# Lattice attention on one core: the product of sine and Gauss term moved to VectorE, all normalisations on GpSimd, and a head's steps laid out on 88 places

## What is computed

```python
scores = einsum('bhqd,bhkd->bhqk', q, k) / sqrt(D_K)      # 64 heads, 1024 x 1024, D_K = 64
int_scores = (abs(scores) * 1618.0).astype(int32)
scores = scores * where(int_scores % 9 in (0, 3, 6), 1/PHI, 1.0)
attn = softmax(scores)
attn = attn * (sin(C1 * attn) * exp(-attn * attn / PHI) + cos(C2 * attn))
ctx = einsum('bhqk,bhkd->bhqd', attn, v)
```

## Time and profile before

| | |
|---|---|
| median of 3 runs | 5791.73 us (5791.23 to 5793.92) |
| profiled execution | 5820.83 us, span 5819.0 us |
| busy, share of the span | PE 82%, DVE 71%, ACT 69%, POOL 65% |
| granted PE clock, mean | 0.944 |

### The profile page before, as it was taken

How to read it: one execution, slowest core, us unless ns; L and a number is a source line. 1 busy time by engine, 2 the same in 40 slices (tenths; PEclk the granted TensorE clock), 3 DMA queues, 4 the chain that set the end, 5 groups by cost and what they waited for, 6 DMA issues and landing times. The chain is left out here.

```text
span 5819.0 us, 98405 instructions
## 1 busy us (share of the span) xinstructions
PE 4780.6 (82%) x27646; PEld 2687.0 (46%) x27689; DVE 4160.0 (71%) x7651; ACT 3990.3 (69%) x5494; POOL 3775.7 (65%) x3599
## 2 busy tenths in 40 slices
PE   2788888888888888888888888888888869996999
PEld 1344444444444444444444444444444436554666
DVE  3677777777777777777777777777777656666665
ACT  1677777777777777777777777777777734444332
POOL 4677777777777777777777777777777634443233
PEclk8899999999999999999999999999999879998999
DMA  1000000000000000000000000000000000000000
GB/s 20 9 8 9 8 10 8 8 8 8 8 8 8 8 8 8 9 8 10 8 8 8 8 8 8 8 8 8 9 8 10 3 9 2 2 2 15 3 6 8
DMA packets 34205, 45.42 MB, mean 8 GB/s; under 512 B 24521, under 2 KB 24585, under 8 KB 34058
## 3 DMA queue, kind: packets, MB, share of 16 engines
q1 hardware_dynamic: 32010, 43.49, 2.8%
q0 software_dynamic: 2048, 0.14, 0.1%
HBM read 39.40 MB, written 4.19 MB: 7 GB/s over the span
## 5 line engine op out<-in xcount | busy, mean ns | idle before, releaser
L617 PE MATMUL banks<-ident,att 128*128 128x128 f32 x8192 | 1145.5, 287 | 408.6 <-DVE ag L549 247.1
L617 PEld LDWEIGHTS banks<-ident,att 128*128 128x128 f32 x8192 | 940.7, 147 | 1003.0 <-DVE ag L549 617.4
L659 PE MATMUL banks<-kT,qT 128*128 128x512 f32 x2048 | 1144.1, 658 | 275.8 <-DVE mx L578 266.5
L419 POOL TENSOR_TENSOR sinb<-sinb,ag 128x1024 f32<-128x1024 f32 x512 | 1280.7, 2505 | 82.7 <-ACT sinb L490 68.9
L569 DVE SCALAR_TENSOR_TENSOR mag<-near,mag 128x512 f32<-128x512 int32 x1024 | 859.6, 844 | 479.3 <-POOL near L435 470.6
L429 POOL TENSOR_SCALAR mag<-mag 128x512 f32<-128x512 f32 x1024 | 689.2, 677 | 567.7 <-DVE mag L569 533.7
L676 PE MATMUL outp<-work,vo 128*64 128x512 f32 x2048 | 1043.4, 634 | 0.0
L676 PE MATMUL outp<-sinb,vo 128*64 128x512 f32 x2048 | 1043.4, 634 | 0.0
L435 POOL TENSOR_SCALAR near<-mag 128x512 int32<-128x512 f32 x1024 | 796.4, 778 | 354.2 <-ACT mag L508 291.5
L508 ACT ACTIVATE mag<-banks 128x512 f32<-128x512 f32 x1024 | 598.7, 592 | 278.0 <-PE banks L659 276.4
L526 DVE TENSOR_TENSOR work<-banks,work 128x1024 f32<-128x1024 f32 x512 | 625.3, 1221 | 190.3 <-ACT work L484 187.7
(11 more groups left out here) (198 smaller groups left out, 6362.8 us busy)
## 6 DMA issues: line engine op xcount, KB each, us to landing
x<-xT_dram SPq DMA_DIRECT2D x128, 256.0 KB, 3.5
xT_dram<-xT SPq DMA_DIRECT2D x8, 256.0 KB
out<-hres SPq DMA_DIRECT2D x8, 256.0 KB, 2.6
base<-in_L_tok_turns,idx POOLq DMA_INDIRECT x64
wqk<-in_L_attn_Wq SPq DMA_DIRECT2D x64, 16.0 KB
wqk<-in_L_attn_Wk SPq DMA_DIRECT2D x64, 16.0 KB
wqk<-in_L_attn_bq SPq DMA_DIRECT2D x64, 0.2 KB
wqk<-in_L_attn_bk SPq DMA_DIRECT2D x64, 0.2 KB
```

Source lines behind the costliest of these rows:

```text
L419: nc.gpsimd.tensor_tensor(sinb[:, k % RING], sinb[:, k % RING], ag[:, k], ALU.mult).then_inc(tmul, 1)
L617: mm = nc.tensor.matmul(turn_pair(k)[:, c, i * P:(i + 1) * P], att[:, p, 4 * half + i, kt * P:(kt + 1) * P], ident[:], is_transpose=True, ...
L659: nc.tensor.matmul(score_bank(n), qT[:, p, (n // 2) * P:(n // 2 + 1) * P], kT[:, p, (n % 2) * 512:(n % 2 + 1) * 512], start=True, stop=Tru ...
```

## The change

The product goes from POOL to DVE. Rows 3 and 7 are normalised by POOL as the others, so `weights2` and `DVE_ROWS` are gone and the transposes wait on `weights` alone. Places are halved: STEPS is 88, and every list and offset is new. The square and the exponential of a Gauss column block and the `ag` product have offsets of their own (SQ, GEXP, AG). Instructions, shapes and buffers stay the same otherwise.

```diff
@@ -300,28 +300,28 @@
         outp = ctx.enter_context(nc.psum_tensor("outp", [P, 512], F32))
 
         names = ("consts loadq loadv projd qk_sb vald v_sb qk mags rounded kept factor filtered bias expd "
-                 "recip weights weights2 turned xpose squared gauss agd cosd acd nned sined tmul av evac folded "
+                 "recip weights turned xpose squared gauss agd cosd acd nned sined tmul av evac folded "
                  "outd").split()
         (consts, loadq, loadv, projd, qk_sb, vald, v_sb, qk, mags, rounded, kept, factor, filtered, bias,
-         expd, recip, weights, weights2, turned, xpose, squared, gauss, agd, cosd, acd, nned, sined, tmul,
+         expd, recip, weights, turned, xpose, squared, gauss, agd, cosd, acd, nned, sined, tmul,
          av, evac, folded, outd) = (sem("l_" + n) for n in names)
 
         NTILE = 2 * TB
         NX = 2 * TB
         HALF = TB // 2
-        STEPS = 44
-        SCORE = [0, 1, 6, 8, 10, 13, 15, 18, 19, 21, 26, 28, 29, 33, 35, 38]
-        ABS, RND, KEEP, FACT, FILT, BIAS = 1, 1, 2, 3, 4, 6
-        EXP = [STEPS + o for o in [4, 5, 7, 8, 9, 13, 15, 16]]
-        GAUSS = [STEPS + o for o in [12, 13, 15, 17, 18, 20, 22, 26]]
-        SINE = [STEPS + o for o in [28, 30, 32, 35, 36, 39, 41, 43]]
-        AV = [STEPS + o for o in [34, 37, 39, 42, 49, 51, 53, 58]]
+        STEPS = 88
+        SCORE = [0, 3, 7, 21, 23, 28, 34, 37, 40, 45, 51, 57, 60, 66, 72, 75]
+        ABS, RND, KEEP, FACT, FILT, BIAS = 2, 2, 5, 6, 9, 23
+        EXP = [STEPS + o for o in [12, 14, 15, 17, 18, 24, 26, 32]]
+        GAUSS = [STEPS + o for o in [24, 25, 30, 31, 38, 41, 43, 46]]
+        SQ, GEXP, AG = 2, 3, 5
+        SINE = [STEPS + o for o in [55, 58, 65, 67, 75, 80, 85, 88]]
+        AV = [STEPS + o for o in [68, 80, 82, 86, 96, 97, 101, 111]]
         OUT = (AV[HALF - 1] + 1, AV[-1] + 1)
-        FOLD, ADD = OUT[1] + 1, OUT[1] + 2
-        PROJ, VAL, EV = (17, 23), 31 + STEPS, 2
-        COS, MUL, RED, SIN, P3 = 1, 1, 3, 3, 4
-        NORM, TURNS = 1, 3
-        DVE_ROWS = (TB // 2 - 1, TB - 1)
+        FOLD, ADD = OUT[1] + 1, OUT[1] + 3
+        PROJ, VAL, EV = (36, 57), 61 + STEPS, 2
+        COS, MUL, RED, SIN, P3 = 1, 2, 6, 6, 9
+        NORM, TURNS = 2, 8
 
         block = ctx.enter_context(nc.Block())
 
@@ -412,13 +412,7 @@
             def iteration(t, par):
                 for s in range(STEPS):
                     for g, p, a in stages(t, par, s):
-                        if a - P3 in SINE:
-                            k = SINE.index(a - P3)
-                            wait(pool, sined, TB * g + k + 1)
-                            wait(pool, agd, TB * (g + 1))
-                            nc.gpsimd.tensor_tensor(sinb[:, k % RING], sinb[:, k % RING], ag[:, k],
-                                                    ALU.mult).then_inc(tmul, 1)
-                        if a - NORM in EXP and EXP.index(a - NORM) not in DVE_ROWS:
+                        if a - NORM in EXP:
                             j = EXP.index(a - NORM)
                             held(pool, recip, TB * g + j + 1)
                             nc.gpsimd.tensor_scalar(att[:, p, j], att[:, p, j], rs[:, j:j + 1], TURN,
@@ -491,8 +485,8 @@
                                                  scale=2.0 * math.pi * (1.0 - 2.0 ** -22)).then_inc(sined, 1)
 
                     for g, p, a in stages(t, par, s):
-                        if a - 1 in GAUSS:
-                            d = GAUSS.index(a - 1)
+                        if a - SQ in GAUSS:
+                            d = GAUSS.index(a - SQ)
                             wait(act, xpose, NX * g + d + 1)
                             if d < RING:
                                 wait(act, av, TB * g - RING + d + 1)
@@ -507,8 +501,8 @@
                             wait(act, filtered, NTILE * g + n - 3)
                             nc.scalar.activation(mag[:, n % 4], score_bank(n), ACT.Abs).then_inc(mags, 1)
                     for g, p, a in stages(t, par, s):
-                        if a - 1 in GAUSS:
-                            d = GAUSS.index(a - 1)
+                        if a - GEXP in GAUSS:
+                            d = GAUSS.index(a - GEXP)
                             wait(act, squared, TB * g + d + 1)
                             nc.scalar.activation(work[:, d % RING], work[:, d % RING], ACT.Exp,
                                                  scale=-1.0 / PHI).then_inc(gauss, 1)
@@ -542,26 +536,24 @@
                             wait(dve, expd, TB * g + j + 1)
                             nc.vector.reciprocal(rs[:, j:j + 1], ssum[:, j:j + 1]).then_inc(recip, 1)
                     for g, p, a in stages(t, par, s):
-                        if a - 2 in GAUSS:
-                            d = GAUSS.index(a - 2)
+                        if a - AG in GAUSS:
+                            d = GAUSS.index(a - AG)
                             wait(dve, gauss, TB * g + d + 1)
                             wait(dve, tmul, TB * (g - 1) + d + 1)
                             nc.vector.tensor_tensor(pair(ag[:, d]), turn_pair(d), pair(work[:, d % RING]),
                                                     ALU.mult).then_inc(agd, 1)
-                        if a - NORM in EXP and EXP.index(a - NORM) in DVE_ROWS:
-                            j = EXP.index(a - NORM)
-                            wait(dve, recip, TB * g + j + 1)
-                            nc.vector.tensor_scalar(att[:, p, j], att[:, p, j], rs[:, j:j + 1], TURN,
-                                                    ALU.mult, ALU.mult).then_inc(weights2, 1)
                         if a - TURNS in EXP:
                             j = EXP.index(a - TURNS)
-                            if j in DVE_ROWS:
-                                wait(dve, weights2, 2 * g + j // 4 + 1)
-                            else:
-                                wait(dve, weights, (TB - 2) * g + j + 1 - j // 4)
                             wait(dve, nned, TB * g)
+                            wait(dve, weights, TB * g + j + 1)
                             nc.vector.tensor_scalar(nturn[:, j], att[:, p, j], ROUND, -ROUND,
                                                     ALU.add, ALU.add).then_inc(turned, 1)
+                        if a - P3 in SINE:
+                            k = SINE.index(a - P3)
+                            wait(dve, sined, TB * g + k + 1)
+                            wait(dve, agd, TB * (g + 1))
+                            nc.vector.tensor_tensor(sinb[:, k % RING], sinb[:, k % RING], ag[:, k],
+                                                    ALU.mult).then_inc(tmul, 1)
                     for g, p, a in stages(t, par, s):
                         if a - KEEP in SCORE:
                             n = SCORE.index(a - KEEP)
@@ -609,8 +601,7 @@
             def fill(g, p, k):
 
                 half = k // HALF
-                wait(pe, weights, (TB - 2) * g + (TB // 2 - 1) * (half + 1))
-                wait(pe, weights2, 2 * g + half + 1)
+                wait(pe, weights, TB * g + TB // 2 * (half + 1))
                 for c in range(2):
                     kt = 2 * k % TB + c
                     for i in range(4):
```

## The result

The changed kernel takes 5765.4 us (median of 6, 5758.5 to 5768.5) where the kernel before takes 5792.3: ratio 0.9948, interval 0.9937 to 0.9959. The forecast was 5540, with a range from 5370 to 5750. It is faster, but by a ninth of the forecast, and outside the range.

The account below looks back on a forecast made before the run. No engine was full; POOL set stage E, ACT nearly filled G, POOL and PE were high in S. Terms -3.3, -2.0 and +1.3 gave 66.0 us a head from 70.0, -252 us over 63 periods: 5540 us, range 5430 to 5700.

Parts of the forecast that it names:

- POOL loses the product's 20 us: POOL drops eight products, gains two normalisations, falls from 51.7 to 34.5 us a head and no longer bounds.
- E, -3.3: Stage from ACT's table load before the exponentials to the first square: falls from 14.5 to 11.2 us a head.
- the half clock goes with the stall: In E, PE's drop to 1.2 GHz ends with its idling behind POOL's product; worth 0.6, inside E's gain.
- E does not shrink: Rival: PE still waits for row 3, now on POOL behind rows 0 to 2; -44 us, 5748 us, chance 0.08.
- G, -2.0: Stage from E's end to the load before the cosines: ACT hands off 2.9 us, 0.9 left for waits; ends 0 and -3.6.
- S, +1.3: Stage from the load before the cosines to the next E: grows to 31.8 us with DVE's products; ends 0 and +7.
- half-piece estimate: In S, each product moved to DVE meets half a POOL piece on average under the SBUF lock: 0.6 us a head.
- DVE's recovery, -3.5: Without POOL's long products, DVE's keeps fall toward 0.69 (-2.5) and turns toward 0.70 (-1.0) us a head.
- so they stay hidden: The x and weight loads on SP move with the projections and cost nothing; uncovered, one would delay a projection once per head.
- second way of adding: Check on the sum: DVE busy 57.4, other waits 4.2, and 4.4 of 12.4 waiting for POOL remaining give 66.0 a head.
- signs that were to show the forecast wrong: E above 13, S above 35, a product mean above 1.6 us, or ACT idle more than 4 us in G.
- slower rival: In S, POOL pieces wait up to 1.22 us for DVE's products, delaying filters; +208 us, 6000 us, chance 0.13.

Follow-up runs that it names:

- e4: Kernel before, on its old grid of 44 places, with only the product of sine and ag moved from POOL to DVE: 5687 us, ratio 0.978.
- e8: Changed kernel, on its grid of 88 places, with the product back on POOL and all rows still normalised by POOL: 6184 us, ratio 1.065 to the kernel before.
- e5: Kernel before, on its old grid of 44 places, with only rows 3 and 7 moved to POOL, the product staying there: ratio 1.034.
- e6: Kernel before, on its old grid of 44 places, with both moves, product to DVE and rows 3 and 7 to POOL: ratio 0.999.
- e7: Changed kernel with the second projection at place 47 in place of 57: ratio 0.989 to the kernel before.
- e15: Changed kernel with waits left out on DVE that an earlier wait of the same head covers, 308 loop instructions for 366: ratio 0.979 to the kernel before.
- e18: Changed kernel with rows 3 and 7 back on DVE and already covered DVE waits left out, 328 loop instructions: ratio 0.984 to the kernel before.
- e1: Changed kernel with rows 3 and 7 normalised by DVE again: ratio 0.995 to the kernel before.
- e14: Kernel before, old grid, with only the product on DVE and already covered DVE waits left out, 326 loop instructions for 384: ratio 0.976.

## Why the prediction was wrong

The forecast was -4.0 us a head and the stages gave -0.46. Of the missing 3.5 us, 1.9 are E's, 1.2 S's and 0.4 G's.

*POOL loses the product's 20 us*: right in kind. e4 and e8 show it, and DVE's waits for POOL, forecast to fall to 4.4 us a head, fell to 4.8.

*E, -3.3*: the step that failed first. It measured -1.4. In the head traced above, "row 0 starts at 4.3, four rows of 1.415 end at 10.0" became 5.2 and 11.4; and "the transposes plus the hand-over to the square take 1.2" became 2.1, as PE had been idle for 3.0 us and was at half clock. The neighbouring head shows how much of this is the clock: there the transposes begin at 11.4 too and the rest takes 1.1, so E is 12.5 at full clock and the late rows alone miss the forecast by 1.3. Two prices in the sum were wrong, then: what stands ahead of row 0, counted at 1.2, where two `mag` pieces beside a product took 2.67 by themselves; and the run of rows, taken at the mean of all rows and not at that of rows beside turns. I had written that the half clock goes with the stall; the stall only changed its cause, from DVE's filter to POOL's row 3.

The forecast also never asked what moving rows 3 and 7 costs against leaving them on DVE, which did one in 1.17: e5 and e6 price that at 3.3 and 1.6 us a head. The rival "E does not shrink" named the mechanism, at 5748 and a chance of 0.08. That its number is the nearest is partly luck: E did shrink, by 1.4, and S took that back, which this rival did not have.

*G, -2.0*: measured -1.6, right within its bounds.

*S, +1.3*: measured +2.5. The half-piece estimate held for the product itself: 1.319 us against 1.23 is 0.7 a head, where 0.6 was forecast. The Trainium skill, "SBUF — State Buffer", section "Who interferes with whom", has a product of two SBUF inputs and a POOL instruction that reads SBUF shut each other out, and the trace agrees: in E the product takes 1.63 us and the two `mag` pieces beside it 2.67. Of the 1.1 us by which S passed 31.8, 0.6 are DVE's busy time there (28.8 us over all heads, forecast 28.2) and 0.5 its waits. The product is not what lengthens S: on the old grid, with both moves (e6), S is 29.93, below the 30.36 of before. The layout is. It puts the second projection there, and without it S measures 31.36 (e7), at the forecast's 31.8, but the time comes back in G.

*DVE's recovery, -3.5*: the keeps were to fall from 0.849 to 0.69 and fell to 0.787; the turns, from 0.827 to 0.70, stayed at 0.831. On the old grid the keeps do fall: in e4

```profile
L569 DVE SCALAR_TENSOR_TENSOR mag<-near,mag 128x512 f32<-128x512 int32 x818 | 557.2, 686 | 138.6 <-POOL near L429 133.8
L563 DVE TENSOR_TENSOR sinb<-sinb,ag 128x1024 f32<-128x1024 f32 x411 | 506.4, 1232 | 0.0
```

keeps take 0.686 and products 1.232. The new order puts slow keeps where there were none, into G. The keeps alone in G and S of one head, before (x6 in each) and after (x7 in each):

```profile
2027.03:2051.55 24.52, 4.02 (x6) 1.00 0.04 11
2051.55:2081.38 29.83, 5.84 (x6) 1.00 0.04 10
2054.91:2078.24 23.33, 6.38 (x7) 0.91 0.00 0
2078.24:2110.24 32.00, 5.11 (x7) 1.00 0.06 17
```

In G a keep went from 0.67 to 0.91 us, in S from 0.97 to 0.73. One of the slow ones, in the next head:

```profile
2123.35 1.63 POOL L429 TENSOR_SCALAR near<-mag 128x512 int32<-128x512 f32 x2
2124.43 1.09 DVE L561 SCALAR_TENSOR_TENSOR mag<-near,mag 128x512 f32<-128x512 int32 x1
```

It starts while a `near` piece runs and ends 0.54 us after it, as the keep of the earlier trace rows did behind POOL's product. So DVE's busy time is 59.6 and not 57.4. With the same two moves on the old grid (e6, 50 heads) it is 57.4, as forecast:

```profile
500.00:4000.00 3500.00, 2851.61 (x15810) 1571.13 (x15806) 2869.14 (x4928) 2742.04 (x3551) 1854.68 (x2001) 0.96 0.03 8
```

So the 2.2 us come with the layout. They are not why the time was missed, though: e6 has the forecast's busy time and still needs 69.9 us a head.

*The loads on SP, "so they stay hidden"*: wrong. The second projection at place 57, four ahead of VAL, lets the load of x go out too late; PE waits 0.9 us a head (45.2 us, above). The prediction had named this as what a missing cover would bring. e7 took that wait away, and won 0.34 to 0.55 in all.

*The sum.* 57.4 + 4.4 + 4.2 = 66.0 stands against 59.6 + 4.8 + 5.0 = 69.4. The second way of adding had the waits for POOL nearly right, the busy time 2.2 and the other waits 0.8 too low. The first way added the stages as if what one gains the kernel gains. That holds on the old grid (e6 to e4: 1.8 in E, 1.6 in the sum) and not on the new one (e15 to e18: 1.6 and 0.4), where G takes 1.0 back with DVE already busy nine tenths of it. Why G and S take back what E gives is only argued, from DVE's busy share; no run that changes the order of G alone was made.

Of the signs that were to show the forecast wrong, E above 13 came in one of the two traced heads (13.45) and not in the mean (12.89), and the other three did not come. They were set too wide for a miss of this size.

The slower rival's mechanism, POOL's pieces blocked by products, exists (`mag` pieces at 2.67 for two) but never came near its price.

## What to carry to other kernels

Price a change that moves two things in opposite directions by parts, and run each part alone: here one part won 2.2% and the other lost 2.1%. When work is moved onto a slower engine, ask first whether someone stands at the end of that very queue; POOL's share of busy time, 50% after the change, did not show it here. Price a run of operations from rows that have the same neighbours, not from the mean of all. And whenever the code of a loop changes, look at the first instruction behind the jump and at the instruction queue's packets before explaining why a good edit brought nothing.

## What the runs showed of the hardware

With loop bodies of 384 or 386 instructions on DVE, five packets of 8 KB were fetched on the instruction queue at each turn, and DVE stood still behind the jump, 0.7 us a turn in e4 and 2.3 in e1. Bodies of 308 to 366 fetched nothing, with one exception: e8's 332, with the same five packets a turn and 4.6 us of standing still. So the number of instructions in DVE's body is not the whole rule, and what else counts was not tried.

Leaving out 58 waits and register instructions per turn of DVE's loop, with every operation kept, was worth 0.5 to 0.75 us a head in the changed kernel (e15), which was not expected, and nothing that can be told on the old grid (e14), where it also ended a fetch.
